# A DLRM tower on one core: table splits that subtract a rounded copy in PSUM, and one bank for the spread of indices

## The reference

```python
e = jnp.stack([tbl_0[ids[:, 0]], ..., tbl_25[ids[:, 25]]], axis=1)
sd = jnp.einsum('bfd,bd->bf', e, dense)
ss = jnp.einsum('bfd,bgd->bfg', e, e)
pairs = ss[:, iu, ju]                      # above the diagonal
z = jnp.concatenate([dense, sd, pairs], axis=1)
h = jnp.concatenate([z, dense], axis=1)
h = jnp.maximum(h @ W_top1 + b_top1, 0.0)  # 607 x 512
h = jnp.maximum(h @ W_top2 + b_top2, 0.0)  # 512 x 256
y = h @ W_top3
```

## Time and profile before

| | us |
|---|---|
| median of 3 runs | 396.62 (396.27 to 397.10) |
| the profiled execution | 395.68 |
| its span, first to last instruction | 393.9 |
| PE (TensorE) busy | 344.1 |
| POOL (GpSimd) busy | 270.6 |
| DVE (VectorE) busy | 240.8 |
| ACT (ScalarE) busy | 182.5 |

### The profile page before, as it was taken

The page is one execution under the profiler, slowest core; times in us unless marked ns, Lnnn a source line. Parts: engine busy times, 40 slices in busy tenths (PEclk is TensorE's granted clock), DMA queues, the critical chain, the costliest instruction groups (busy, mean ns, idle before and its releaser), DMA issues.

```text
span 393.9 us, 12374 instructions
## 1 busy us (share of the span) xinstructions
PE 344.1 (87%) x5434; PEld 262.5 (67%) x5434; DVE 240.8 (61%) x466; ACT 182.5 (46%) x280; POOL 270.6 (69%) x279
## 2 busy tenths in 40 slices
PE   5799977887999998798999998799999988545996
PEld 1566655765788875586788875687788865435773
DVE  1799993685898643686998642588997541101420
ACT  3544155783223227775223338575133258932333
POOL 6788887777777777777777777777777777770000
PEclk9999996999999999999999999899999999958899
DMA  7995113243343223343333214243333122110000
GB/s 193 258 260 144 40 42 116 66 108 81 78 109 87 55 53 76 96 116 85 96 97 87 53 47 123 59 115 84 108 80 85 53 61 56 52 55 17 2 2 0
DMA packets 20089, 33.41 MB, mean 85 GB/s; under 512 B 7907, under 2 KB 10467, under 8 KB 20037
## 3 DMA queue, kind: packets, MB, share of 16 engines
q0 software_dynamic: 8704, 17.84, 18.0%
q1 hardware_dynamic: 11333, 14.78, 14.0%
HBM read 32.60 MB, written 0.01 MB: 83 GB/s over the span
## 4 chain that ended last, share of the span: by engine, by line
PE 45%; POOL 34%; issue 14%; DMA 3%; ACT 2%; DVE 1%; POOLq 0%; ACTq 0%; DVEq 0%
POOL rows L440 34%; PE late_bank L533 9%; PE gram_bank L500 7%; PE late_bank L461 6%; PE late_bank L462 5%; PE turn_bank L481 5%; PE turn_bank L461 3%; PE turn_bank L462 3%; DMA rows<-in_tbl_dram,index 2%; PE spare_bank L567 2%; PE gram_bank L567 1%; PE late_bank L578 1%; ACT turned L324 1%; PE turn_bank L514 1%; PE gram_bank L514 1%
## 5 line engine op out<-in xcount | busy, mean ns | idle before, releaser
L440 POOL DMA_INDIRECT rows<-in_tbl_dram,index x272 | 269.8, 992 | 84.1 <-issue 80.8
L803 DVE TENSOR_TENSOR one_hot<-table_ids,row_number 125x512 fp32r<-125x512 int32 x216 | 133.7, 681 | 24.9 <-PE turn_bank L462 15.6
L324 ACT COPY turned<-turn_bank 128x512 f32<-128x512 f32 (+1 forms) x72 | 70.6, 1029 | 43.8 <-PE turn_bank L481 39.6
L461 PE MATMUL late_bank<-one_hot,table_hi 125*128 125x512 f32 x192 | 81.0, 422 | 3.8 <-DVE table_lo L875 3.4
L462 PE MATMUL late_bank<-one_hot,table_lo 125*128 125x512 f32 x192 | 76.7, 399 | 0.0
L481 PE MATMUL turn_bank<-ident,rows 128*128 128x128 f32 x288 | 47.5, 298 | 23.7 <-DMA rows<-in_tbl_dram,index 13.7
L500 PE MATMUL gram_bank<-turned 128*27 128x26 f32 x4096 | 55.1, 195 | 13.3 <-issue 13.0
L500 PEld LDWEIGHTS gram_bank<-turned 128*27 128x27 f32 x4096 | 45.6, 108 | 29.7 <-issue 27.4
L481 PEld LDWEIGHTS turn_bank<-ident,rows 128*128 128x128 f32 x288 | 35.0, 151 | 35.5 <-issue 16.1
L295 DVE COPY gram<-gram_bank 124x208 f32<-124x208 f32 x32 | 12.0, 374 | 69.9 <-PE gram_bank L500 69.8
L461 PEld LDWEIGHTS late_bank<-one_hot,table_hi 125*128 125x128 f32 x192 | 36.6, 191 | 17.0 <-DVE table_lo L875 5.0
(11 more groups left out here) (74 smaller groups left out, 327.6 us busy)
## 6 DMA issues: line engine op xcount, KB each, us to landing
table_ids<-in_ids_by_table_dram SPq DMA_DIRECT2D x27, 256.0 KB, 3.3
rows<-in_tbl_dram,index POOLq DMA_INDIRECT x272
turned<-in_tbl_dram SPq DMA_DIRECT2D x6, 448.0 KB, 11.7
looked_up<-in_tbl_dram SPq DMA_DIRECT2D x3, 448.0 KB, 5.1
rows<-in_r_dense_features_dram SPq DMA_DIRECT2D x16, 64.0 KB, 2.8
gram<-in_W_top_dram SPq DMA_DIRECT2D x1, 702.0 KB
gram<-in_W_top_dram SPq DMA_DIRECT2D x1, 512.0 KB
turned<-in_tbl_dram SPq DMA_DIRECT2D x6, 52.0 KB
```

The lines of the kernel that those rows point to most:

```text
L324: copy(to[:, f0:f1], of).then_inc(rows_copied[n % 2], 1)
L440: pool.indirect_dma_start(out=rows[:, row % RING_ROWS, :], out_offset=None, in_=tables[f], in_offset=bass.IndirectOffsetOnAxis(ap=index[:, ...
L461: pe.matmul(bank, table_hi[:, s, k, :], hot, start=k == 0, stop=False)
L803: last = nc.vector.tensor_tensor(hot, table_ids[0:RK, (c * LOOKUPS + s) % ID_SLOTS, :], row_number[0:RK, k:k + 1].broadcast_to([RK, CHUNK] ...
```

## The change

Each table's rounded copy is now written three times by ScalarE: twice with 512 columns into the two `gram_bank`s in PSUM, as float32r, and then, as before, into `table_hi`. VectorE subtracts the copy in PSUM from the raw table in two halves of 512 columns. Since there is one such pair of banks, `round_table(s)` waits for the split of table s-1. TensorE, which until now knew from `lo_made` that `table_hi` was there, waits for `hi_made` too. The `gram_bank`s are no longer free for the spread of indices, which gets `spare_bank` alone: `spread_ids(s)` waits until the indices of table s-1 have been copied, two spreads are issued first (the second behind the first's copy), and spread s+2 follows look-up s. ScalarE's order changes with it: copy of indices 1 before rounding 1, and rounding s+1 instead of s+2 in the loop.

```diff
-ID_BANKS = 3
+ID_BANKS = 1
...
         def id_bank(s):
-            return free_bank[s % ID_BANKS][0:RK, :]
+            return spare_bank[0:RK, :]
...
-            for s in range(ID_BANKS):
-                spread_ids(s)
+            spread_ids(0)
+            spread_ids(1)
             for s in range(LOOKUPS):
                 pe.wait_ge(lo_made, s + 1)
+                pe.wait_ge(hi_made, s + 1)
                 look_up(0, range(s * K_ROWS, (s + 1) * K_ROWS))
-                if s + ID_BANKS < LOOKUPS:
-                    spread_ids(s + ID_BANKS)
+                if s + 2 < LOOKUPS:
+                    spread_ids(s + 2)
...
                 act.wait_ge(table_loaded[s], DMA)
                 act.wait_ge(table_rest_loaded[s], DMA)
+                if s > 0:
+                    act.wait_ge(lo_made, s)
+                for half in range(2):
+                    nc.scalar.copy(gram_bank[half][0:RK, :].bitcast(F32R), raw[s][:, half * BANK:(half + 1) * BANK]).then_inc(hi_shown, 1)
                 nc.scalar.copy(table_hi[:, s].rearrange("p k d -> p (k d)"), raw[s]).then_inc(hi_made, 1)
...
             round_table(0)
             copy_ids(0)
+            copy_ids(1)
             round_table(1)
-            copy_ids(1)
             round_table(2)
-            round_table(3)
             for s in range(2, LOOKUPS):
                 copy_ids(s)
                 if s - 2 == LOOKUPS - 3:
                     act.wait_ge(w1_merged, 1)
                 copy_found(0, range((s - 2) * K_ROWS, (s - 1) * K_ROWS))
-                if s + 2 < LOOKUPS:
-                    round_table(s + 2)
+                if s + 1 < LOOKUPS:
+                    round_table(s + 1)
...
-                dve.wait_ge(hi_made, s + 1)
-                nc.vector.tensor_tensor(table_lo[:, s].rearrange("p k d -> p (k d)"), raw[s],
-                                        table_hi[:, s].rearrange("p k d -> p (k d)").bitcast(F32), ALU.subtract).then_inc(lo_made, 1)
+                low = table_lo[:, s].rearrange("p k d -> p (k d)")
+                for half in range(2):
+                    cols = slice(half * BANK, (half + 1) * BANK)
+                    dve.wait_ge(hi_shown, 2 * s + half + 1)
+                    last = nc.vector.tensor_tensor(low[:, cols], raw[s][:, cols], gram_bank[half][0:RK, :], ALU.subtract)
+                last.then_inc(lo_made, 1)
```

More of the change, by code:

```diff
@@ L218, in dlrm_tower @@
         hi_made = sem("hi_made")
+        hi_shown = sem("hi_shown")
         lo_made = sem("lo_made")
```

## The result

| | before | after |
|---|---|---|
| median | 396.29 us (6 runs) | 392.24 us (6 runs, 389.72 to 394.13) |
| ratio to before | | 0.9901, 95% interval 0.9872 to 0.9929 |
| span of the profiled execution | 393.9 | 389.6 |

The forecast was 392.3 us, with a range of 390.6 to 395.6, and 389.6 us for the span. The sum came out. Its terms did not all have the size that I gave them: the gathers gained more than I had put down, the first ring wait took some of it again, and the two made up for each other.

The account below looks back on a forecast made before the run. POOL's never-empty queue of indirect gathers was taken as the bound. A gain of 4.3 us took the span from 393.9 to 389.6, the profiled execution to 391.4; adding 0.94 for the median gave 392.3 us, range 390.6 to 395.6.

Parts of the forecast that it names:

- the first ring wait: POOL's gather at 65.13 needs TensorE's first four transposes: slack 6.65 us, less delay 1.8, caps POOL's gain at 4.85.
- the prologue's losses: Between the gathers of 2.90 and 61.38, POOL loses 11.0 us against its undisturbed pitch of 1.25 us.
- The size of that gain: POOL's gain over nine table splits once the subtraction reads PSUM: 4.3 us, between 3.5 and 6.1.
- the 0.44 a table: Gain for eight tables: a gather's loss of 0.68 us beside the split, less 0.24 for one-hots that stay.
- My sign: Evidence to look for in the prologue: the gather of 61.38 would start near 57.1.
- The caps: Limits on POOL's lead: 4.85 us at the first ring wait, 4.2 from TensorE's own gather waits, 5.25 at a later ring wait.
- The third cap: At the gather of 321.67, TensorE's lead of 4.2 plus slack 1.03 lets POOL be at most 5.25 us ahead.
- The tail: What follows the last gather stays unchanged; a stretch at the lower clock could shift time up to 1.6 us either way.
- TensorE's delay d: TensorE leaves the prologue 1.8 us later: 1.1 for table 0's copies, 0.1 for VectorE's split, 0.6 for the last spread.
- Nothing happens: Rival, chance 0.11: POOL gains nothing in the prologue and TensorE's delay is absorbed, 396.6 us.
- Part of it arrives: Rival, chance 0.17: TensorE leaves the prologue 3.5 us late, so the ring cap cuts the gain; 393.5 to 395.6 us.
- Lock-step: Rival, chance 0.06: ScalarE's chain doesn't fit beside a table, TensorE waits every table; 400.1 us, slower from 0.6 us growth each.

Follow-up runs that it names:

- e3: The changed kernel with a ring of 46 rows instead of 44: 389.99 us, ratio 0.9825 to the kernel before.
- e7: The changed kernel with the subtraction in one instruction of 1024 columns reading the rounded copy from two neighbouring PSUM banks: 393.19 us, ratio 0.9913.
- e2: The kernel before with only the change's order and single bank; table split uncut, both inputs in SBUF, PSUM banks written once: 395.31 us, ratio 0.9977.
- e1: The changed kernel, but VectorE's halves subtract the rounded copy in SBUF instead of the one in PSUM: 392.47 us, ratio 0.9912.
- e4: The changed kernel, but table 0 is split from SBUF in one instruction without its copies into PSUM: 391.90 us, ratio 0.9872.

## Why the prediction was right, and where it was not

**POOL's queue is the bound, and the prologue's losses are never made up: right.** e3 shows it best, where POOL is 5.6 us ahead behind the prologue and 5.8 at its end.

**The input in SBUF holds gathers up: right**, shown by e7 against e2, 9.9 to 3.5 us with one instruction of the same length in both, and by the gathers that start 0.51 us behind a split, 0.68 against nothing. The inference that I quoted from the Trainium skill (SBUF — State Buffer, "Who interferes with whom"), that the descriptors of such a DMA would not be held by a `tensor_tensor`, disagrees with these runs; its rule that two SBUF inputs contend with a GpSimd instruction that reads SBUF agrees, if the gather's reading of its indices counts as that, which no run here tests.

**The size of that gain: too small.** I took 4.3 us, of bounds 3.5 and 6.1. The loss fell by 9.4 - 4.1 = 5.3, 0.59 a table instead of 0.48. The term that was mis-sized is the 0.44 a table, above all its subtraction of 0.24 for one-hots that "stay". The 0.68 of the gather of 26.94 is what was left of the split, 0.71, with no share of one-hots in it, and with the input in PSUM a gather at that place loses nothing. Nor did eight tables lose 0.68: the gathers that met the nine splits lost 0.28, 0.26, 1.04, five times 0.68, and 0.59, 5.6 in sum, of which 5.3 went. The 0.39 of L337, which made 0.44 look like the cleaner number, is the price of another instruction. I also left out that halves alone would save something; here they didn't add to it.

My sign that the gather of 61.38 would start near 57.1 missed too: it started at 54.30. But the 7.1 us there, and the 5.85 by which POOL was ready earlier for the gather of 65.13 (59.28), overstate the gain. At the same gather, the kernel before has the weight splits and L337 behind it, and the changed one has not.

**The caps: right in kind, and the first one decided.** I had worked out 4.85 us for the first ring wait, and 4.99 passed it (65.13 - 60.14): the slack of 6.65, less a delay of 1.39 and less 0.27 from the end of the first four transposes (59.24 + 0.63) to the gather. POOL stood still for 60.14 - 59.28 = 0.86. Of the 4.99 another 0.75 was owed: the gather of 60.14 took 1.69 instead of 0.94 beside the weight split and L338, and e3, without the wait, pays there too (1.43 and 1.32 for the gathers of 58.67 and 61.65). So the gain was 5.85 - 0.75 = 5.1, near the 5.3 of the loss; the wait took 0.86 of it, and 4.24 is what is left at the 45th gather and what arrived (4.08 and 4.17 later). I had set the cap against the whole gain, without what is owed.

The third cap, TensorE's lead and the slack of 1.03, I put at 5.25; it stood at 4.3. TensorE's first transposes of the last chunk were ahead by 320.01 - 316.45 = 3.56 instead of 4.2, and of the slack all but 0.27 was used, 3.56 + 0.76 = 4.32 = 321.67 - 317.35. It took nothing from the time, though it looks as if it had decided: POOL was only 4.08 ahead when it came there. It waited 0.21 and the gather took 1.13 instead of 0.94, but before, the gather of 319.97 had lost 0.46 beside L337, and the changed kernel's at that place (315.89) lost nothing. One gather later both stand as they stood, 322.92 - 318.78 = 4.14. A part of the missing 0.6 went in the third chunk, at whose start the lead was still 233.80 - 229.74 = 4.06. There an idle stretch of TensorE that the profile calls issue had grown from 2.98 to 3.65 us. The longest such stretch is between 2.5 and 4.3 in the kernels measured here, whatever their ring and split, so I can't put it down to the change.

```profile
244.94 0.87 PE L501 MATMUL gram_bank<-turned 128*27 128x26 f32 x56 [3.65 <-issue]
```

So 4.3 was not a gain of 4.3 that passed under all caps. It was one of 5.1 that the first ring wait cut to 4.24. That the mis-sized term and the cut came to the forecast's number is luck. In e7, POOL was ready even 7.2 us ahead (56.31 + 1.29 + 0.30 = 57.90) and stood still for 3.1 of them. A sum that comes out is no proof of its terms.

```profile
56.31 1.29 POOL L442 DMA_INDIRECT rows<-in_tbl_dram,index  x1 [0.30 <-issue]
60.99 1.69 POOL L442 DMA_INDIRECT rows<-in_tbl_dram,index  x1 [3.40 <-PE turn_bank L483]
```

**The tail: unchanged, as said.** From the last wait for a gather to the end it was 393.9 - 354.45 = 39.45 us before and is 389.6 - 350.13 = 39.47 after. The stretch of the lower clock level moved with the work (granted clock 0.59 from 364 to 368 before, 0.62 from 360 to 364 after) and cost nothing new.

**TensorE's delay d: 1.39 against 1.8.** The copies before the first look-up cost 1.05 (7.24 to 8.29), as forecast, but the first table had landed 0.5 us earlier in that execution, so that the first look-up moved by 0.45 only. From there to the first transposes it lost 0.94; I had said 0.7 (0.6 and 0.1). The last spread stands at 48.18, behind look-up 6, where I had put it, and the wait for VectorE before look-up 8 (54.40) was 1.17.

**The rivals.** Nothing happens: refuted by loss and time. Part of it arrives: the ring wait that it names is what ran, but with d at 1.39 instead of 3.5 and a larger gain. Lock-step: the splits at 27.03 and 32.13 are 5.10 us apart, against a pitch of 4.98 before, so a table grew by 0.1 and not by the 0.6 from which this case would decide.

## What to carry to other kernels

Where GpSimd issues indirect DMAs all the time, look at each of VectorE's instructions with two inputs in SBUF beside them: one input in PSUM gives the time back to the queue, and a cut in two, if no bank is free, gave about a third of it here. Before booking it, list the waits of that queue with their slack, and keep a running lead of each engine against it: the smallest slack caps the gain. Read the lead behind the stretch that changed: inside it, costs that one kernel has paid and the other has not look like gain. A buffer of a few rows more was worth another 2 us here (392.24 to 389.99), though alone it was worth nothing. And test a right forecast as one tests a wrong one; the experiment that seemed to refute mine (e1) did so only in the time, while the gathers' loss had moved as it should.

## What the runs showed of the hardware that I had not expected

- Two halves of 0.68 us that lie back to back hold gathers up less than one instruction of 1.22 (loss 6.0 and 6.8 against 9.4 us over nine tables), with the same inputs; four of 0.42 in sum no less than two (7.3).
- A gather that starts within a table split with both inputs in SBUF (1.22 us) is held until the split ends: it lost 0.68 us when 0.71 were left, and 1.04 when 1.08 were left. The copy L337, with 0.84 left, cost 0.39. In the kernel before, gathers and tables fell into step, and five tables in a row (from 26.43 on) cost 0.68 each.
- One VectorE instruction may read 1024 columns across two neighbouring PSUM banks, in 1.21 us, as long as the same from SBUF (1.22).
- TensorE's first matmuls are 0.43 us apart, the later ones 0.23. A look-up that began 1.0 us earlier (e4) did not reach the faster pace earlier (16.8 against 16.1 us), so only 0.25 us of the 1.0 was left at the first transposes.
